# Second layer of a fused transformer kernel: order of two scales on GpSimd, another pair of engines for the last four normalisations, and a finer sort

## The reference, cut to what matters

```
x = x + LN(attention16heads(LN(x)))                     # first layer
n = LN(x)
y = LN(n + mha4heads(n)) * g1 + be1                     # second layer, attention part
e = argmax(y @ Wg.T)                                    # one of 8 experts for every token
z = LN(y + relu(y @ W1[e] + b1[e]) @ W2[e] + b2[e]) * g2 + be2
out = x + LN(z)
```

## Time and profile before

| | |
|---|---|
| median of 3 runs | 632.38 us (627.19, 632.38, 633.19) |
| the profiled execution's own time | 633.14 us |
| its span | 631.4 us |
| PE / DVE / ACT / POOL busy | 83% / 69% / 56% / 51% of the span |
| mean granted TensorE clock | 0.911 |
| `second_attention`: first scale on POOL to last copy of row numbers | 338.8 to 496.4 us |
| `experts`: first PE instruction | 513.27 us |

### The profile page before, as it was taken

How to read it: one execution, slowest core, us unless ns; L and a number is a source line. 1 busy time by engine, 2 the same in 40 slices (tenths; PEclk the granted TensorE clock), 3 DMA queues, 4 the chain that set the end, 5 groups by cost and what they waited for, 6 DMA issues and landing times. The chain is left out here.

```text
span 631.4 us, 15860 instructions
## 1 busy us (share of the span) xinstructions
PE 522.1 (83%) x5164; PEld 378.9 (60%) x5164; DVE 438.8 (69%) x1253; ACT 354.8 (56%) x957; POOL 322.1 (51%) x542
## 2 busy tenths in 40 slices
PE   2899999999999999999964898888875149999910
PEld 2576666666665655666633676666664149999910
DVE  2265888888888878888742777787775506888860
ACT  1215566767676655777641797776651025767750
POOL 5140244443355547612234557778888700377776
PEclk9999999999999988999985899999776559999965
DMA  4200523001011101011120000000000222244333
GB/s 106 77 2 2 169 70 49 15 20 20 19 20 19 21 18 19 4 20 19 20 51 17 35 2 2 1 3 10 20 30 28 86 56 68 34 59 64 31 31 33
DMA packets 38099, 21.62 MB, mean 34 GB/s; under 512 B 13433, under 2 KB 36353, under 8 KB 38018
## 3 DMA queue, kind: packets, MB, share of 16 engines
q1 hardware_dynamic: 18544, 10.65, 7.4%
q0 software_dynamic: 6640, 4.92, 5.6%
q10 hardware_dynamic: 12834, 5.04, 3.2%
HBM read 10.11 MB, written 8.12 MB: 29 GB/s over the span
## 5 line engine op out<-in xcount | busy, mean ns | idle before, releaser
L331 DVE TENSOR_REDUCE nmax<-psA 128x2 f32<-128x512 f32 x256 | 164.8, 685 | 63.6 <-PE psA L209 63.1
L493 ACT ACTIVATE pr<-psB 128x512 f32<-128x512 f32 x250 | 136.0, 595 | 95.1 <-PE psB L226 95.0
L209 PE MATMUL psA<-km,qp 24*128 24x256 f32 x768 | 129.0, 432 | 2.2 <-DVE nmax L331 1.7
L226 PE MATMUL psB<-q,km 26*128 26x256 f32 (+1 forms) x752 | 112.7, 416 | 0.2 <-DMA q<-mT 0.2
L209 PEld LDWEIGHTS psA<-km,qp 24*128 24x128 f32 x768 | 81.3, 200 | 34.9 <-DVE nmax L331 23.2
L1595 POOL DMA_INDIRECT out<-wz,ys x39 | 63.4, 1627 | 54.5 <-ACT wz L1550 45.7
L586 POOL TENSOR_TENSOR km<-kraw,rows_of 128x768 f32<-128x768 f32 x16 | 23.5, 1467 | 122.8 <-ACT kraw L468 114.9
L226 PEld LDWEIGHTS psB<-q,km 26*128 26x128 f32 (+1 forms) x752 | 70.1, 192 | 1.3 <-DMA q<-mT 0.6
L240 PE MATMUL psO<-pr,v 128*32 128x256 f32 x1024 | 70.0, 392 | 0.1
L1163 ACT ACTIVATE prob<-psS,nbias 128x128 f32<-128x128 f32 x128 | 45.5, 382 | 12.7 <-DVE nbias L992 12.7
L1451 DVE TENSOR_TENSOR hT<-psH,e_nb1T 128x512 f32<-128x512 f32 x39 | 27.0, 692 | 30.2 <-PE psH L1412 22.2
(11 more groups left out here) (196 smaller groups left out, 1115.3 us busy)
## 6 DMA issues: line engine op xcount, KB each, us to landing
q<-mT SPq DMA_DIRECT2D x256, 1.0 KB
ys<-y_sorted SPq DMA_DIRECT2D x39, 72.0 KB, 1.9
e_w<-W ACTq DMA_DIRECT2D x1, 2048.0 KB
e_w<-W ACTq DMA_DIRECT2D x4, 512.0 KB
xs<-x_all SPq DMA_DIRECT2D x16, 128.0 KB
out<-x_all SPq DMA_DIRECT2D x15, 128.0 KB, 3.7
x_all<-x SPq DMA_DIRECT2D x1, 1536.0 KB, 8.5
out<-wz,ys POOLq DMA_INDIRECT x39
```

The lines of the kernel that those rows point to most:

```text
L209: last = T.matmul(psA[:, (16 * b + n) % 3, c * L1:(c + 1) * L1], query_part(b, h, depth, c), keys(b, h, depth, slice(0, L1)), start=True, ...
L226: last = T.matmul(bank_of(b, h)[:, c * L1:(c + 1) * L1], keys(b, h, depth, slice(c * P, (c + 1) * P)), queries(b, h, depth, slice(0, L1)), ...
L331: V.tensor_reduce(nmax[:, b % 2, hf, :, at], psA[:, (16 * b + n) % 3, :].rearrange("p (c m) -> p c m", c=2), AX.X, ALU.max, negate=True).t ...
L493: A.activation(pr[:, h % PRING, :, :].rearrange("p c l -> p (c l)"), bank_of(b, h), ACT.Exp, scale=SCALE1).then_inc(S["b_free"], 1)
```

## The change

Three things change, all in `second_attention`.

1. On POOL `ready_x(t + 1)` stands directly behind `add_bo(t)`, ahead of the closing normalisation of step t - 6.
2. For t = 18 to 21 (`rooted`), which is steps 12 to 15, POOL does no normalisation. ACT takes a square root of the variance at the start of its iteration (`late_norm`), DVE takes the reciprocal and minus mean times it (`late_scales`, behind the maxima and ahead of the residual), and ACT then applies scale and bias to the two tiles. `finish_y` stays on DVE from t = 16 on, now behind the residual's statistics.
3. The third part of eight tiles is cut into two of four, so there are six parts; the sorts are at t = 12, 16, 18, 20, 22 and behind the loop. Sends are 2, 2, 2, 2, 2, 3, 3, 4, 4, 0, 4 in t = 13 to 23, where they were 2 in each of t = 13 to 21, then 6 and 4.

```diff
-CHUNKS = ((0, 8), (8, 8), (16, 8), (24, 4), (28, 4))
-SORT_AT = {12: 0, 16: 1, 20: 2, 22: 3}
-SEND_AT = {13: (0, 0, 2), 14: (0, 2, 2), 15: (0, 4, 2), 16: (0, 6, 2), 17: (1, 0, 2), 18: (1, 2, 2), 19: (1, 4, 2),
-           20: (1, 6, 2), 21: (2, 0, 2), 22: (2, 2, 6), 23: (3, 0, 4)}
+CHUNKS = ((0, 8), (8, 8), (16, 4), (20, 4), (24, 4), (28, 4))
+SORT_AT = {12: 0, 16: 1, 18: 2, 20: 3, 22: 4}
+SEND_AT = {13: (0, 0, 2), 14: (0, 2, 2), 15: (0, 4, 2), 16: (0, 6, 2), 17: (1, 0, 2), 18: (1, 2, 3), 19: (1, 5, 3),
+           20: (2, 0, 4), 21: (3, 0, 4), 23: (4, 0, 4)}
...
+        eps = sb("eps2", [P, 1])
+        sd_y, nb_y = sb("sd_y", [P, 2]), sb("nb_y", [P, 2])
+        SETS = NSTEP - 4
...
+        def rooted(t):
+            return t >= NSTEP + 2
...
+            def late_scales(i, n):                                     # DVE
+                dve.wait_ge(S["yln_step"], 3 * i)
+                dve.wait_ge(S["sd_ok"], i - SETS + 1)
+                V.reciprocal(rs_y[:, :], sd_y[:, :]).then_inc(S["late_step"], 1)
+                dve.wait_ge(S["late_step"], i - SETS + 1)
+                V.scalar_tensor_tensor(out=nb_y[:, :], in0=mv_y[:, n, :, 0], scalar=-1.0, in1=rs_y[:, :],
+                                       op0=ALU.mult, op1=ALU.mult).then_inc(S["yln_step"], 1)
...
-                if late(t) and has(t, 6):
-                    finish_y(t - 6, m % 2, t)
+                if rooted(t) and has(t, 6):
+                    late_scales(t - 6, m % 2)
                 if has(t, 5):
...
                     last.then_inc(S["yagg"], 1)
+                if late(t) and has(t, 6):
+                    finish_y(t - 6, m % 2, t)
...
+            def late_norm(i, n):                                       # ACT
+                act.wait_ge(S["yagg"], i + 1)
+                act.wait_ge(S["consts"], 2)
+                act.wait_ge(S["late_step"], i - SETS)
+                A.activation(sd_y[:, :], mv_y[:, n, :, 1], ACT.Sqrt, bias=eps[:, :]).then_inc(S["sd_ok"], 1)
+                act.wait_ge(S["yln_step"], 3 * i + 1)
+                for c in range(2):
+                    last = A.activation(yn[:, c, :], r2[:, n, c, :], ACT.Identity, bias=nb_y[:, c:c + 1],
+                                        scale=rs_y[:, c:c + 1])
+                last.then_inc(S["yln_step"], 1)
             def iteration(t, m):
+                if rooted(t) and has(t, 6):
+                    late_norm(t - 6, m % 2)
...
+                G.memset(eps[:, :], EPS)                               # POOL, once
...
                 if has(t, 0):
                     add_bo(t, m % 2)
+                if has(t + 1, 0):
+                    ready_x(t + 1, (m + 1) % 2)
...
-                if has(t, 6):
+                if has(t, 6) and not rooted(t):
...
-                if has(t + 1, 0):
-                    ready_x(t + 1, (m + 1) % 2)
```

More of the change, by code:

```diff
@@ L815, in second_attention @@
                  "rd_ok", "pn_ok", "pt_full", "pt_ok", "al_full", "att_ok", "lg_ok", "yst", "yagg", "ystep",
-                 "yln_step", "y_ok", "ids_ok"]
+                 "yln_step", "sd_ok", "late_step", "y_ok", "ids_ok"]
         S = {n: ctx.enter_context(nc.semaphore("l2_" + n)) for n in names}
```

## The result

| | before | after |
|---|---|---|
| median | 631.0 us (18 runs, 626.29 to 633.19) | 625.43 us (18 runs, 622.46 to 627.93) |
| profiled execution, its own time / span | 633.14 / 631.4 us | 626.56 / 624.8 us |
| mean granted TensorE clock | 0.911 | 0.905 |

A forecast was written before the change was run, and what follows sets the result against it. POOL was taken to set the pace from iteration 6 on. -7.3 (loop) and +3.1 (late iterations) gave -4.2, or -6.8 with a quick end: 628.2 or 625.6 against the median, said as 627, range 620 to 633.

The forecast's parts named there:

- Steady iteration: Second attention from iteration 6 on: POOL stays the bound, an iteration falls from 7.84 to 7.12 us.
- ACT's ring: Next bound behind POOL in steady iterations: the loop of ACT and PE, at 6.61 us an iteration.
- Collisions: POOL and DVE blocking each other in steady iterations: 0.84 us of each 7.12, taken as unchanged.
- rivals of 3.8 us lost and 3.6 us gained by collisions: DVE divisions block POOL fully, 7.66 us an iteration, 631 (chance 0.15); or cost nothing, 623.5 (chance 0.17).
- -7.3 us by iteration 17: Early x scale on POOL, iterations 6 to 17: DVE begins iteration 17 about 7.3 us earlier.
- +3.1 for the exchange: Iterations 18 to 23: ACT and DVE waiting on each other for the late normalisations loses 3.1 us, between 1.8 and 4.5.
- Table load: ACT, start of iteration 18: 1.28 us load, covered by 2.8 us of DVE's mark and divisions.
- Part 3, "no gain by itself, since SP's zeros end later": End of block: six parts leave fewer sends after the last row numbers, but SP's zero blocks end later than POOL's queue.
- My two ends: End of block: 2.6 us gained if zero issues become quick, nothing if they stay slow; even chance.
- The slow end: Rival, end of block: ACT's and SP's zero issues stay slow, giving 628.5 us; chance 0.2.
- The long exchange: Rival, iterations 18 to 21: each costs 3 us more than counted, +12 in all, giving 640 us; chance 0.1.
- The early scale does nothing: Rival, loop: DVE can't run ahead, so moving the x scale gains nothing, giving 633 to 635 us; chance 0.03.

The follow-up runs named there:

- part 1 alone: Kernel before with only POOL's x scale moved ahead of the closing normalisation: 630.0 us, ratio 0.9988 to the kernel before.
- SP alone: Kernel before with all eight zero blocks issued by SP and none by ACT: 629.64 us, ratio 0.9999 to the kernel before.

## Why the prediction was right or wrong

The time, 627, is near the measured one by luck: two errors cancel, the loop's gain (4.2 us said, none found in the profile) and the end's (2.6 said, 5.8 found).

- **Steady iteration: right on average.** 7.12 predicted, 7.15 measured; ACT's ring 6.61 predicted, its xy copies at 380.40 and 386.99 (iterations 7 and 8) are 6.59 apart, still with 0.87 of wait for PE. POOL's idle went as said.
- **Collisions: right in size, other in place.** The scale's small instructions are short now, and the two divisions fall on the closing `y_all` and on `add_bo`: 1.06 and 1.18 instead of 0.73 each, 0.78 us in sum for the 0.84 I kept. But DVE is held too: a division of 0.69 takes 0.95 and 1.02, and three small additions of the sort take 1.76 at 419.63, beside POOL's two `y` products, and 0.74 at 455.63, beside a send. The rivals of 3.8 us lost and 3.6 us gained by collisions fell with this. The Trainium skill, page "SBUF — State Buffer", section "Who interferes with whom", has such blocking in both directions; the trace agrees as to the directions, and these rows don't show whether one blocks the other whole.
- **-7.3 us by iteration 17: wrong, and the step that failed.** It is 2.35 in the trace, and part 1 alone is worth 0.1% of the time, not 1.2%. The 7.3 came from a walk whose steps the prediction doesn't show. Two things failed. I took the sort of iteration 12 as it stood, with POOL as the bound; with POOL faster, DVE's sort is the bound, and POOL waits 2.29 us. And I bounded the ring by rows at full clock only; faster iterations came with a lower clock (in part argued, see above). My 8.4 us for iterations 15 and 16 came to 3.5 (`psXY` at 450.06 against 453.52). Two of my sums are also off by a little: 453.52 - 445.2 is 8.3, and 466.2 with 3.9 more is 470.1, not 470.3.
- **+3.1 for the exchange: right** (28.13 - 25.70 = 2.4, inside its 1.8 to 4.5). PE's matmuls don't take half the time at full clock, as I wrote, but 0.6 of it: the four for the logits 0.61 us at 401.59 after, and 1.02 at 401.55 with part 1 alone, at the low clock. From copy to copy iteration 18 takes 7.8 us, where my walk has 7.9, and iteration 19 takes 7.0, where it has 2.0 + 4.9. But I did not ask whether `probT` has to stand behind the stop. It need not, and that is 4.6 us of these iterations, more than the exchange cost.
- **Table load: as said.** 464.35, covered; the root begins at 465.64, right behind 464.35 + 1.28. The Trainium skill, page "ScalarE: Activation LUTs", section "What ACT_TABLE_LOAD costs", adds a drain of about 1.38 us. Between load and root there is none here.
- **Part 3, "no gain by itself, since SP's zeros end later": wrong.** I read the end from one execution in which the zeros took 10.5 us. In the five other profiles with seven or eight sends behind the last row numbers they take 4.1 to 4.5, or 8.5 for eight blocks, and from the last row numbers to PE it is 14.6 to 15.8 us, beside 16.9 in the profile before. Then POOL's drain is last (8.03 measured, 7.6 predicted), and each send less is worth up to 1.26 us: from 14.7 to 11.1 is 3.6 us typical. Against my one profile it reads as 5.8. Against SP alone, which is the kernel before with quick zeros, PE begins the experts 4.2 us earlier in block time (168.5 and 172.7). My two ends were -2.6 and 0; the quick end was the right one, but too small.
- **Rivals.** The slow end fell: it is in none of the other profiles, part 1 alone with the same backlog and the same two issuers included. The long exchange fell: 2.4 us more, not 11. "The early scale does nothing" had a chance of 0.03, and for the time it is nearly what the experiment gave, though by another way: DVE does run ahead. That it was worth so little is open in part, since the clock's share is argued.

## What to carry to other kernels

When a stage is bound by one engine, price the next bounds at the granted clock that they may have, and look for the iterations that are not steady (here a sort), since those take the gain back first. Ask of an engine that works in order which of its instructions has its input ready: moving `probT` ahead of a stop took 4.6 us out of the late iterations and brought the ratio from 0.9922 to 0.9887 (the intervals just touch), nearly half of what the whole change gave. Read the end of a block from the last instruction that nobody can overlap, here POOL's last send, and check in a second execution whether a slow stretch is there at all.

## What was not expected of the hardware

- An indirect DMA send costs POOL 1.26 us (0.96 and 0.30 of issue), and the queue is free 3.9 to 4.1 us after the start of the last one, in every profile with quick zeros.
- 48 memsets of one column on POOL hold one DVE cast for 1.14 us instead of 0.17 (457.52), and it is 0.17 again when they are moved.
- TensorE's clock fell to 1.2 GHz in the middle of steady iterations (block time 61.5 to 70.0) in seven of nine profiles with the shorter iteration and in none of the five others. With part 1 alone it fell behind a gap of 0.64 us in front of y's transposes at 400.08, and in the other six it fell within 0.6 us of such a gap too (0.63 or 0.64 us); after has the same gap at 400.65 (0.63 us), and its clock stayed full.
- SP's and ACT's zero blocks took 2.7 us an issue in one execution and 0.9 to 1.1 in all others, five of them with as many sends or more waiting on POOL.
